# An image and text fusion block on one core: new order lists, a one-value maximum, a buffer of its own for z, and the first squares in h2

## The reference, cut to what matters

```python
def tok(img):                       # patches of 16x16, (B,196,768)
    x = layernorm(patches(img), g1, b1) @ W + b
    return layernorm(x, g2, b2)     # (B,196,256)
h = concat([tok(x), txt], axis=1)   # (64,273,256)
# attention of each row over its own 16 heads (16 values each), not over the rows
h = h + attn(layernorm(h))          # Q,K,V = x@W+b; softmax(Q K^T / 4) V; @Wo + bo
# token mixing with the row before (zeros before row 0)
z = layernorm(h); prev = shift(z)
xr = mu_r*z + (1-mu_r)*prev; xk = mu_k*z + (1-mu_k)*prev
h = h + sigmoid(xr @ Wr.T) * (square(relu(xk @ Wk.T)) @ Wv.T)
```

## Time and profile before

| | before |
|---|---|
| timed runs, median of 3 | 1629.72 us (1624.85 to 1634.03) |
| the profiled execution | 1621.5 us |
| its span, first to last instruction | 1619.8 us |
| TensorE busy | 1451.5 us, 90% |
| VectorE busy | 1203.4 us, 74% |
| ScalarE busy | 1107.2 us, 68% |
| GpSimd busy | 1023.6 us, 63% |
| mean granted TensorE clock | 0.965 |

### The profile page before, as it was taken

One profiled execution on the slowest core, in us unless ns is written; L12 is line 12 of the kernel. 1 busy time (PEld: TensorE's weight loads), 2 busy tenths in 40 slices (PEclk: granted clock), 3 DMA queues, 4 the chain that ended last, 5 costly groups with the idle time before them and its releaser, 6 DMA issues. The chain is left out here.

```text
span 1619.8 us, 53760 instructions
## 1 busy us (share of the span) xinstructions
PE 1451.5 (90%) x18762; PEld 1383.3 (85%) x18762; DVE 1203.4 (74%) x3075; ACT 1107.2 (68%) x2230; POOL 1023.6 (63%) x1524
## 2 busy tenths in 40 slices
PE   4687899899989999999999999999999999988866
PEld 4677899798988989898999989998898889987756
DVE  5575787787867778787788868887778777877642
ACT  4554677677767777777777767777677677766643
POOL 3333567576666766766676766767676676666556
PEclk9798999999999999999999999999999999999988
DMA  5278889877977887797799788897888779778751
GB/s 137 53 144 137 129 157 147 135 149 154 159 132 150 143 148 159 160 148 163 136 151 162 145 151 137 171 161 136 158 148 150 144 151 154 152 132 130 132 79 38
DMA packets 702660, 227.67 MB, mean 141 GB/s; under 512 B 617470, under 2 KB 673854, under 8 KB 702394
## 3 DMA queue, kind: packets, MB, share of 16 engines
q1 hardware_dynamic: 702394, 224.23, 77.3%
HBM read 121.64 MB, written 89.64 MB: 130 GB/s over the span
## 5 line engine op out<-in xcount | busy, mean ns | idle before, releaser
L1048 PE MATMUL bank<-wqkv,xnT 128*126 128x384 f32 (+1 forms) x1728 | 359.1, 348 | 31.9 <-DVE h L877 22.9
L1048 PEld LDWEIGHTS bank<-wqkv,xnT 128*126 128x126 f32 (+1 forms) x1728 | 294.1, 185 | 44.0 <-issue 35.7
L1128 PE MATMUL bank<-wtok,xT 128*98 128x258 f32 x2304 | 314.9, 293 | 8.2 <-DVE xT L787 7.4
L1128 PEld LDWEIGHTS bank<-wtok,xT 128*98 128x98 f32 x2304 | 293.3, 172 | 11.2 <-DVE xT L787 8.5
L684 POOL TENSOR_TENSOR mixp<-mixf,mixp 128x364 fp32r<-128x364 f32 x192 | 183.6, 975 | 163.8 <-ACT mixp L1022 163.1
L943 ACT ACTIVATE arena<-qk,ymask 128x768 f32<-128x768 f32 x192 | 164.1, 930 | 72.9 <-DMA qk<-qkv_dram 72.9
L863 DVE TENSOR_TENSOR qkvt<-bank,bqkv 126x384 f32<-126x384 f32 (+1 forms) x288 | 156.0, 545 | 46.6 <-PE bank L1048 45.1
L632 POOL TENSOR_TENSOR xcols<-xcols 84x896 f32<-84x896 f32 x64 | 135.3, 2113 | 69.1 <-ACT xcols L977 68.3
L672 POOL TENSOR_TENSOR dT<-zT 128x364 f32<-128x364 f32 x96 | 75.2, 793 | 145.1 <-ACT zT L1016 144.9
L964 ACT ACTIVATE xcols<-xim 84x640 f32<-84x640 f32 (+1 forms) x192 | 129.6, 694 | 16.4 <-DVE xs L782 16.0
L621 POOL TENSOR_TENSOR rs<-ve,small 126x3 f32<-126x3 f32 (+1 forms) x160 | 129.2, 807 | 12.5
(11 more groups left out here) (122 smaller groups left out, 3320.3 us busy)
## 6 DMA issues: line engine op xcount, KB each, us to landing
xim<-in_x SPq DMA_DIRECT2D x128, 294.0 KB
qk<-qkv_dram SPq DMA_DIRECT2D x48, 768.0 KB, 7.6
qkv_dram<-qkvt SPq DMA_DIRECT2D x96, 378.0 KB
arena<-qkv_dram SPq DMA_DIRECT2D x384, 48.0 KB, 3.9
qkv_dram<-qkvt SPq DMA_DIRECT2D x48, 336.0 KB
o_dram<-probs SPq DMA_DIRECT2D x288, 48.0 KB, 1.9
out<-h SPq DMA_DIRECT2D x96, 126.0 KB
on<-o_dram SPq DMA_DIRECT2D x64, 126.0 KB
```

Source lines behind the costliest of these rows:

```text
L1048: ins = mm(psum, left(a, k), right(b, k), start=t == 0, stop=t == len(terms) - 1)
L1128: ins = mm(place("tok", c)[0:PT, 0:E + 2], xT[:, a, i0:i0 + GRID // 2, :].rearrange("p i w -> p (i w)"), wtok[:, b, ch, :], start=t == 0, ...
```

## The change

- `AT` and `BANK` get new numbers: the order of the work on each engine and queue, and the banks.
- z gets a buffer of its own, and the two waits that the shared buffer needed are gone.
- The two copies into qx become reductions with a maximum over one value: the same result from another instruction.
- The squares of images 0 to 4 are written into h2 (`aside`). xcols of images 1 to 5 then waits for the transposes and the square of the image before, not for `ssq`. The squares wait for `ssq` of the image before (one buffer for all), the first for `ready`, and the first residual add for the fifth image's `ssq`.

```diff
-AT = dict(load=[0], xcols=[1555, 1687, 1876], sq=[3679], ssq=[4380], sqm=[4077, 4754], x=[2492, 2687, 2748],
...
-    h=[7672, 8038], hdma=[9674], st3=[12693, 12843, 12966], mv3=[12988, 13082, 13112], rstd3=[13465], xn=[13777,
...
-    qk_in=[17953], v_in=[19005], qplace=[19042, 19048], kspread=[19082, 19222, 19230, 19256], s=[19435, 19452],
...
-    av=[20075, 20094], rec=[20283, 20307], osb=[20293, 20332], o_out=[21113], o_in=[25935], ont=[26318, 26698],
-    onh=[26409, 26726], onl=[26493, 26925], wo=[27035, 27261, 27330], h2=[27208, 27323, 27365], st4=[27324, 27769,
...
+AT = dict(load=[0], xcols=[1286, 1360, 1572], sq=[3289], ssq=[4033], sqm=[4154, 4522], x=[2233, 2262, 2325],
+    xh=[2346, 2509, 2855], xl=[2437, 2890, 3072], tok=[3483, 4281], stat=[4290], statc=[4342], statr=[4356],
+    rstd1=[4876], txt=[8203], yn=[5071, 5080], st2=[6096, 6614], mv2=[6412, 6745], rstd2=[7116], hg=[6689, 7135],
+    h=[7151, 7277], hdma=[8401], st3=[12212, 12374, 12755], mv3=[12779, 12881, 12893], rstd3=[13150], xn=[13428,
...
+    15625, 15962, 15965], qb=[14929, 15093, 15671, 15727, 16040, 16073], qkv_out=[15524, 17019, 17289],
+    qk_in=[17928], v_in=[19407], qplace=[18710, 18904], kspread=[18610, 18648, 18721, 18823], s=[18976, 19119],
...
+    av=[19692, 19783], rec=[19729, 19843], osb=[19823, 19872], o_out=[21287], o_in=[25703], ont=[25824, 25848],
+    onh=[25980, 26179], onl=[26168, 26231], wo=[26599, 26759, 26889], h2=[26751, 26867, 26931], st4=[27289, 27297,
...
+BANK = dict(x=[5, 3, 1], tok=[3, 1], stat=[5], yn=[7], xt=[6, 0], qkv=[0, 6, 0, 2, 0, 2], s=[2, 4], pt=[4, 6],
+    av=[4, 6], ont=[5, 2], wo=[6, 2, 5], zt=[6, 4], k=[0, 4], r=[0, 2, 5], val=[2, 0, 5])
...
-        z = on
+        z = sb("z", [TT, TILES, E])
...
-        x_sq = isig("x_sq", 1)
+        x_sq = isig("x_sq", 1, True)
...
+        EARLY = 5
+        aside = h2[0:XROWS, :, :, :].rearrange("p c i e -> p (c i e)")[:, 0:GRID * 128]
+
+        def squares(n):
+            return aside if n < EARLY else xcols[:, :]
...
-                        after(z_pe, q, k - 1, 2)
...
-                            q_sb.done(V.tensor_copy(qx[half, :, xx, :], qk[half, :, 0:HD]))
+
+                            q_sb.done(V.tensor_reduce(qx[half, :, xx, :], qk[half, :, 0:HD].unsqueeze(3), AX.X, ALU.max))
...
+                            if q * CPQ + k == 0 and i == 0:
+                                x_stats.wait(dve, 0, EARLY - 1, 1)
...
-                                x_stats.wait(act, q, k - 1, 1)
+                                if q * IPQ + k <= EARLY:
+                                    x_tr.wait(act, q, k - 1, 3)
+                                    x_sq.wait(act, q, k - 1, 1)
+                                else:
+                                    x_stats.wait(act, q, k - 1, 1)
...
+                        if n < EARLY:
+                            x_stats.wait(act, q, k - 1, 1)
+                        if n == 0:
+                            act.wait_ge(ready, 1)
+                        x_sq.done(A.activation(squares(n), xcols[:, :], ACT.Square))
...
-                            on_pe.wait(act, q, k, 2)
```

More of the change, by code:

```diff
@@ L69 @@
-BANK = dict(x=[5, 1, 3], tok=[1, 3], stat=[5], yn=[7], xt=[2, 4], qkv=[4, 5, 4, 6, 0, 2], s=[0, 6], pt=[2, 0],
-    av=[2, 5], ont=[6, 0], wo=[5, 0, 6], zt=[4, 6], k=[5, 2], r=[0, 5, 2], val=[0, 2, 0])
+AT = dict(load=[0], xcols=[1286, 1360, 1572], sq=[3289], ssq=[4033], sqm=[4154, 4522], x=[2233, 2262, 2325],
+    xh=[2346, 2509, 2855], xl=[2437, 2890, 3072], tok=[3483, 4281], stat=[4290], statc=[4342], statr=[4356],
+    rstd1=[4876], txt=[8203], yn=[5071, 5080], st2=[6096, 6614], mv2=[6412, 6745], rstd2=[7116], hg=[6689, 7135],
+    h=[7151, 7277], hdma=[8401], st3=[12212, 12374, 12755], mv3=[12779, 12881, 12893], rstd3=[13150], xn=[13428,
+    13605, 13663], xt=[13790, 14108], xnh=[14103, 14209], xnl=[14200, 14339], hb=[15380], qkv=[14837, 14929, 15308,
+    15625, 15962, 15965], qb=[14929, 15093, 15671, 15727, 16040, 16073], qkv_out=[15524, 17019, 17289],
+    qk_in=[17928], v_in=[19407], qplace=[18710, 18904], kspread=[18610, 18648, 18721, 18823], s=[18976, 19119],
+    mx=[19109, 19173], sub=[19193, 19208], exp=[19467, 19489], pt=[19492, 19585], ptc=[19622, 19691, 19718, 19722],
+    av=[19692, 19783], rec=[19729, 19843], osb=[19823, 19872], o_out=[21287], o_in=[25703], ont=[25824, 25848],
+    onh=[25980, 26179], onl=[26168, 26231], wo=[26599, 26759, 26889], h2=[26751, 26867, 26931], st4=[27289, 27297,
+    27355], mv4=[27483, 27496, 27591], rstd4=[27778], z=[27938, 27946, 27953], zt=[28011, 28082], carry=[27118],
+    ztc=[28060, 28229], d=[28266, 28362], edge=[28742], mix=[28894, 28919, 29680, 29788], mixh=[29091, 29254, 29711,
+    31008], mixl=[29260, 29474, 30682, 31486], k=[29687, 29913], kr=[29857, 30972], ksq=[31172, 31497], kah=[31206,
+    31847], kal=[31708, 31911], r=[32313, 32463, 32853], rt=[32529, 32890, 32963], val=[33078, 33316, 33437],
+    rv=[33165, 33606, 33775], add=[34429, 34606, 34925], out=[34967, 35584, 36135], sqh=[3887])
@@ L630, in body @@
                         x_sq.wait(pool, q, k, 1)
-                        halves = xcols[:, :].rearrange("p (w a q) -> p a w q", a=2, q=64)
+                        halves = squares(q * IPQ + k).rearrange("p (w a q) -> p a w q", a=2, q=64)
                         x_half.done(P.tensor_tensor(halves[:, 0, :, :], halves[:, 0, :, :], halves[:, 1, :, :], ALU.add))
@@ L781, in body @@
                         settle(dve)
-                        x_stats.done(V.tensor_reduce(xs[:, :], xcols[:, :].rearrange("p (w q) -> p w q", q=128)[:, :, 0:64], AX.X, ALU.add))
+                        x_stats.done(V.tensor_reduce(xs[:, :], squares(q * IPQ + k).rearrange("p (w q) -> p w q", q=128)[:, :, 0:64], AX.X, ALU.add))
                     for job, (w0, w1) in enumerate(XCUT):
@@ L973, in body @@
                     for k in due(q, s, "sq", 0):
+                        n = q * IPQ + k
                         x_tr.wait(act, q, k, 3)
                         x_cols.wait(act, q, k, 3)
-                        x_sq.done(A.activation(xcols[:, :], xcols[:, :], ACT.Square))
+                        if n < EARLY:
[3 more added lines that the diff above has]
+                        x_sq.done(A.activation(squares(n), xcols[:, :], ACT.Square))
                     for c in range(2):
```

10 lines of the change are left out of this document (removed).

## The result

The changed kernel takes 1677.77 us (median of 4 runs, 1672.39 to 1678.78) against 1631.88 for the kernel before beside it: a ratio of 1.028 (95% interval 1.024 to 1.032), 46 us slower. The forecast was 1633, with 1608 to 1652 as its range: the measured time lies 26 us above its upper end.

A forecast was written before the change was run, and what follows sets the result against it. TensorE was taken to bound the middle, 94% busy, with a DMA chain within 1 or 2 us of it. Terms 0 - 2 + 0 + 5 + 1 - 1 = +3 us gave 1633 us on the median, range 1608 to 1652.

The forecast's parts named there:

- term (b): Queue behind qk, one chunk in three: a text copy added ahead of the value loads; +1 us, bounds 0 and +8.
- term (a): Patch copies between qkv's last third and the load of on, at another chunk: +5 us, bounds -16 and +20.
- R2: Slower rival: patch-copy delay at 5401 felt whole, 0.4 us for value loads; +20 us, 1650 us, 22%.
- TensorE's busy time: Whole kernel: the forecast is wrong if this time itself moves by over 10 us.
- The maximum: One-value reductions into qx: 945 ns each, long copies gone; -2 us, bounds -17 and +21.
- R3: Slowest rival: the one-value maximum into qx takes 4 us; about +150 us, 3%.
- Early squares: Fill, first five images' squares in h2: taken as 0, bounds -16 and +3 us.
- my own test: Fill: fifth image's token matmuls within 2 us of before; 10 us earlier would prove the early squares right.
- z buffer: Drain: last load of on leaves some 12 us earlier, its transposes do not; 0 us.
- Term (c): Last chunk: one GpSimd instruction less ahead of the low part of mix; -1 us, bounds 0 and -2.
- Waits for h: TensorE's waits for VectorE's h, 17.4 us before: under 10 us, part handed to the score matmuls.
- R1: Faster rival: TensorE's waits for h and on shrink to a third; -20 us, 1610 us, 28%.

The follow-up runs named there:

- e1: Changed kernel with its value loads at 18201 instead of 19407, right behind qk and any image load; 1.0145 of the kernel before.
- e14: Changed kernel with its value loads at 18402 instead of 19407, still behind text load and patch copies in one chunk; 1.0148 of the kernel before.
- e15: Changed kernel with its patch copies at 9750 instead of 8401, value loads left in place; 0.9896 of the kernel before.
- e2: Kernel before with its value loads at 19675 instead of 19005, behind the patch copies in one chunk of three; 0.9885 of the kernel before.
- e19: Changed kernel with patch copies at 9750 and the one-value maximum turned back into the copy; 0.9895 of the kernel before.
- e18: Kernel before with one code edit alone, the one-value maximum in place of the copy; 1.0092 of the kernel before.
- e9: Kernel before with its value loads at 19340 instead of 19005; 1.0030 of the kernel before.
- e20: Kernel before with its patch copies at 9940 instead of 9674, behind the loads of on; 0.9932 of the kernel before.
- e10: Kernel before with one code edit alone, the first five images' squares in h2; 1.0032 of the kernel before.
- e7: Changed kernel with the patch copies alone moved from 8401 to 8950; 1.0271 of the kernel before.
- e12: Changed kernel with its value loads at 19190 instead of 19407; 1.0312 of the kernel before.
- e13: Changed kernel with value loads at 18201 and transposes of on at 25920 and 25925 instead of 25824 and 25848; 1.0204 of the kernel before.
- e17: Second measurement of the kernel before with its value loads at 19675 instead of 19005; 0.9918 of the kernel before.

## Why the prediction was wrong

**Value loads, term (b): the step that failed.** It said that the value loads leave 2.7 us ahead of their matmuls, that the new order adds "a text copy, a few tenths", +1 us, bounds 0 and +8. Measured: 34.3 us of waits, and moving these loads alone gives back 1.35% (e1 and e14), 22 of the 46 us. The order named in that step was right: text, four copies, output, image load, value loads. What is added ahead of the loads was right too: they leave 0.6 us later behind qk (10.55 against 9.92). The price was wrong three times. I left out that the loads themselves take longer to issue right behind the image load: 7.64 us on average, in the chunk of the earlier trace rows 5.84. I took the distance to the matmuls as unchanged, and it is 0.5 us shorter on average (18.86 against 19.32). And I took the 2.7 us between the last issue and the matmuls for slack. It was none: in that kind of chunk the loads land 2.9 us behind the last issue on average, so the earlier trace rows showed a load that was already just in time. 2.4 us of lateness (18.20 against 15.76) came on top of nothing. Nor was it the same chunk: the value loads at 3407 are those that stood at 3005 before, ahead of text and copies, where the issue ended at 14.40; they moved by 3.8 us.

**The patch copies, term (a).** Forecast +5, bounds -16 and +20. In the changed kernel the waits for on, 13.5 us, are less than the 16.2 of before; by that count the term is harmless. Yet with the value loads in time the waits for on are 25.2 us (e1) and 31.9 (e14), and both kernels are still 1.5% (24 us) slower than before. If all of that is the copies', which no run isolates against the place of before, the term was worth 24 us, a little over its upper bound. The place of 9750 is another matter: e15 lies 2.5% (41 us) below e14, more than going back to the order of before would give. The term was masked, because TensorE stood waiting for the value loads and came late to on as well. R2's mechanism fits: in the changed kernel the waits for on rose from 5.0 to 10.3 us in the chunk at 5703 and fell only from 9.9 to 7.3 in the chunk that the copies left. But it put the value loads at 0.4 us.

**TensorE's busy time.** "Wrong if it moves by over 10 us": it moved by 19.2, and the granted clock accounts for it. The forecast had no term for it. One of the waits and what followed it, windows of 5 us (length, then TensorE's busy time; the granted clock is third from last):

```profile
750.00:755.00 5.00, 1.81 (x50) 1.52 (x52) 0.63 (x2) 3.18 (x7) 3.50 (x5) 0.91 0.86 173
755.00:760.00 5.00, 5.00 (x81) 4.76 (x72) 3.73 (x9) 0.14 (x1) 0.90 (x2) 0.75 0.40 110
760.00:765.00 5.00, 5.00 (x44) 4.89 (x43) 3.85 (x15) 3.54 (x10) 3.35 (x8) 1.00 0.54 133
```

TensorE stands still for 3.19 us until 753.75, and then part of two windows runs at 1.2 GHz; the value matmuls behind the wait took 3.10 us, in e15 1.88. Nine of the 17 pieces at the lower clock in the middle begin within 2 us of the end of a wait of 3.0 to 4.1 us ahead of value matmuls. The busy time does not simply go with the sum of the gaps: 1124.1 us at 62.3 of gaps (e2), 1136.0 at 73.0 (before), 1148.9 at 108.8 (lists alone), 1153.8 at 105.6 (after), but 1135.4 at 58.9 (e15) and 1135.9 at 85.7 (e14). Of the middle, 17.1 us ran at the lower clock in e14 and 41.0 us in e1, both with no wait for value loads. So the late value loads cost a second time, through the clock; what other waits cost through it differs from run to run, and no rule comes out of these runs.

**The maximum.** 945 ns forecast, 947 measured, none long: right, and R3 (4 us) is out. The copies of the same lists, in e19, spread from 542 to 2448 ns, the maxima from 932 to 953. What the Trainium skill says (SBUF — State Buffer, "Who interferes with whom"), that a copy in a two-port mode can be locked out by GpSimd and a tensor_reduce never is, agrees with these rows. The gain that it would allow did not come: e19 and e15 are equal. The scores start when ScalarE's four copies are through, and the second maximum ends just ahead of them, in the chunk shown above at 743.60 against 743.78:

```profile
740.37 3.41 ACT L951 ACTIVATE arena<-qk,ymask 128x768 f32<-128x768 f32 x4 [1.58 <-DMA qk<-qkv_dram]
742.65 0.95 DVE L855 TENSOR_REDUCE qx<-qk 64x768 f32<-64x768 f32 x1
```

The row of the scores at 743.88 names the maximum, though ScalarE's last copy ended 0.18 us later. For TensorE the -2 us was near 0 with these lists, and +15 with the old ones (e18).

**Early squares: 0.** Right. The fifth image's token matmuls came at 80.3 us, before 83.7, which by my own test spoke for some effect; e9 and e20 have 80.5 and 81.1 without the edit, e10 82.5 with it. The test was too narrow for how the fill varies.

**z buffer: 0.** The last load of on leaves at 1628.21 and its transposes run at 1645.91, 17.7 us apart, before 6.7: 11 us earlier, as forecast, and the transposes gain nothing. Term (c) could not be told apart: from the first scores of chunk 45 to the end it is 121.8 us, before 124.2, and 120.3 to 128.1 in the other runs.

**Waits for h** were to be under 10 us and are 15.4: wrong. They are between 2.4 (e7) and 15.7 us (e12) in every run with the new lists but e13. The banks and the image work of the new lists were not tried apart; with the copies at 9750 no loss is left that they would have to explain.

**The chances.** 26% for slower was what the two signs of R1 and R2 gave. It was too little: the forecast's sum let signs cancel over margins (2.7 us, 1 to 2 us) of which none had been measured against a landing, and it held no term for the clock, which made the waits of the changed kernel dearer.

## What to carry to other kernels

Read a DMA queue for each kind of chunk apart, from the issue of the large load to the last issue, and set that against the time at which the matmuls could start, less the landing. A margin between issue and use is not slack until the landing is taken off. The place of four small copies, 3.3 us of issue, was worth 2.5 to 3.9% (e14 and after, against e15); and a move that repeats at another period than the chunk (3000 against 4000 steps here) has to be checked in every chunk, which I failed to do twice. When a wait goes away, expect the next one to show: the waits for on nearly doubled when the value loads were in time (13.5 to 25.2 us).

## What the hardware showed that I had not expected

The first DMA issued right behind the 768 KB load takes long to issue, whichever it is: 4.23 us for the text load in the chunk shown, 4.13 in that of e15, and 5.89 us for the two image loads in the earlier trace rows's chunk before. In the middle stretches of all twenty traces a text, image, patch or value load that comes first there takes 4.0 to 6.3 us, an output store 0.3 to 4.9 us. A text load takes 0.30 us elsewhere (753.83 in the kernel after). The eight value loads take 9.86 us right behind it (e1, at 774.06), and the mean of that kind of chunk is 10.02 us. The same eight loads take 5.5 to 6.0 us behind the patch copies and 7.6 to 8.3 right behind the 588 KB of the image load (means by run). The issue time of a DMA is thus no constant of the DMA: it goes with what was issued before it. What in the queue or the DMA engines holds it was not tried.

The fill of kernels that differ only in orders or code that comes later takes one of two lengths: the second image's token matmuls begin at 35.5 to 35.9 us in nine profiles and at 37.9 to 38.8 in eleven, and no single edit separates them. The only kernel profiled twice (e2 and e17) had the long one both times (38.0 and 38.6), so whether one and the same kernel takes both is not shown. What sets it was not tried.
